# Nine small start-up loads of a four-layer cross-attention kernel issued from other engines' queues

## The reference, cut to what matters

```python
# layer 0: attention over the 256 features ("time"), 64 channels
Mn = Wn @ inorm(x) + bn;  Mm = Wm @ inorm(ctx) + bm;  Ml = Wl @ ctx + bl
A = softmax(einsum('bct,bcs->bts', Mn, Mm))
x = Wo @ einsum('bcs,bts->bct', Ml, A) + bo + x
# layers 1 and 2: 16 heads of 16 over the 64 rows, masked keys
a = layer_norm(ctx, ln_gamma, ln_beta)
Q, K, V = x @ Wq.T, a @ Wk.T, a @ Wv.T
x = x + tanh(gate) * (softmax(where(mask, Q K^T / 4, -inf)) V) @ Wo.T
# layer 3: one head of 256
x = x + alpha * (softmax((x w_q^T)(ctx w_k^T)^T / 16) (ctx w_v^T)) w_o^T
```

## Time and profile before

| | us |
|---|---|
| median of 3 runs | 601.56 |
| lowest, highest | 598.97, 601.84 |
| the profiled execution, device time | 601.84 |
| its span | 600.0 |
| PE busy in it | 564.3 (94%) |
| DVE, ACT, POOL busy | 473.7, 463.4, 120.5 |
| mean granted TensorE clock | 0.990 |
| start of PE's first matmul | 6.64 |
| start of `nT` on PE (L463), prologue | 21.65 |

### The profile page before, as it was taken

The page is one execution under the profiler, slowest core; times in us unless marked ns, Lnnn a source line. Parts: engine busy times, 40 slices in busy tenths (PEclk is TensorE's granted clock), DMA queues, the critical chain, the costliest instruction groups (busy, mean ns, idle before and its releaser), DMA issues.

```text
span 600.0 us, 26503 instructions
## 1 busy us (share of the span) xinstructions
PE 564.3 (94%) x11087; PEld 497.5 (83%) x11087; DVE 473.7 (79%) x1063; ACT 463.4 (77%) x961; POOL 120.5 (20%) x138
## 2 busy tenths in 40 slices
PE   3898999999999999999999999999999999999875
PEld 2687897988898897988889888988889888888864
DVE  4786969787897969878798869878797869877654
ACT  2675969878897869877797869878788778869661
POOL 8410070103410070102501060101601052000000
PEclk9989999999999999999999999999999999999979
DMA  9320000210021000210020100210020100010001
GB/s 218 107 77 2 2 3 14 68 38 2 2 78 34 7 2 3 78 37 2 2 78 3 37 2 2 78 38 2 2 78 2 38 1 3 3 38 1 2 3 36
DMA packets 18273, 18.36 MB, mean 31 GB/s; under 512 B 1552, under 2 KB 18064, under 8 KB 18176
## 3 DMA queue, kind: packets, MB, share of 16 engines
q1 hardware_dynamic: 17072, 16.19, 8.8%
q0 software_dynamic: 768, 0.45, 0.5%
q10 hardware_dynamic: 336, 0.20, 0.2%
HBM read 12.63 MB, written 4.19 MB: 28 GB/s over the span
## 4 chain that ended last, share of the span: by engine, by line
PE 76%; ACT 11%; DVE 6%; issue 4%; DVEq 0%; ACTq 0%
PE psum L383 13%; PE psum L673 11%; PE psum L727 10%; PE psum L385 10%; PE psum L384 10%; ACT work L854 5%; PE psum L720 5%; PE psum L640 4%; PE psum L653 3%; ACT v L803 3%; PE psum L520 2%; PE psum L463 2%; DVE shifted L1031 2%; PE psum L448 1%; DVE negmax L1027 1%
## 5 line engine op out<-in xcount | busy, mean ns | idle before, releaser
L1027 DVE TENSOR_REDUCE negmax<-psum 128x8 f32<-128x512 f32 x128 | 87.3, 682 | 11.2 <-PE psum L653 11.2
L1031 DVE TENSOR_TENSOR shifted<-psum,negmax 128x512 f32<-128x512 f32 x128 | 88.5, 692 | 5.3
L868 ACT ACTIVATE work<-psum,group_mask 128x512 f32<-128x512 f32 x128 | 80.4, 698 | 10.0 <-PE psum L673 9.6
L854 ACT ACTIVATE work<-shifted 128x512 f32<-128x512 f32 x128 | 75.5, 631 | 3.3 <-DVE shifted L1031 2.0
L673 PE MATMUL psum<-const,work 64*128 64x64 f32 x1536 | 64.9, 228 | 11.9 <-ACT work L854 9.2
L673 PEld LDWEIGHTS psum<-const,work 64*128 64x128 f32 x1536 | 56.2, 141 | 23.7 <-ACT work L854 14.9
L727 PEld LDWEIGHTS psum<-v,work 128*64 128x64 f32 x2048 | 63.0, 138 | 7.6 <-issue 3.0
L727 PE MATMUL psum<-v,work 128*64 128x34 f32 x2048 | 67.6, 225 | 0.8 <-ACT work L868 0.8
L803 ACT ACTIVATE v<-psum 64x256 f32<-64x256 f32 x128 | 49.6, 388 | 20.2 <-PE psum L385 19.1
L849 ACT ACTIVATE work<-psum,negmax 128x256 f32<-128x256 f32 x128 | 50.7, 483 | 3.8 <-DVE negmax L1023 3.7
L795 ACT ACTIVATE kbd<-psum,own_bias,const 128x512 f32<-128x512 f32 x64 | 46.6, 791 | 0.6 <-PE psum L385 0.6
(11 more groups left out here) (187 smaller groups left out, 1527.9 us busy)
## 6 DMA issues: line engine op xcount, KB each, us to landing
x_raw<-in_x_dram SPq DMA_DIRECT2D x8, 512.0 KB, 4.4
c_raw<-in_ctx_dram SPq DMA_DIRECT2D x8, 512.0 KB, 5.4
out_dram<-attn SPq DMA_DIRECT2D x16, 256.0 KB, 2.2
kbd<-in_L_xattn_Wq_dram SPq DMA_DIRECT2D x2, 256.0 KB, 9.0
kbd<-in_L_xattn_Wk_dram SPq DMA_DIRECT2D x2, 256.0 KB, 9.3
kbd<-in_L_xattn_Wv_dram SPq DMA_DIRECT2D x2, 256.0 KB, 10.2
kbd<-in_L_xattn_Wo_dram SPq DMA_DIRECT2D x2, 256.0 KB, 11.3
mrow_u<-in_mask_dram SPq DMA_DIRECT2D x7, 64.0 KB, 4.9
```

What stands on the lines that cost most here:

```text
L854: act.activation(probs[:, exp_row(g, l, i, last), :], shifted[:, i % 4, :], ACT.Exp).then_inc(exps, 1)
L868: act.activation(probsT[:, at, :], o[:], ACT.Copy, scale=group_mask[:, 2 * i + c:2 * i + c + 1]).then_inc(free, 1)
L1027: dve.tensor_reduce(negmax[:, i % 2, :], sv, AX_X, ALU.max, negate=True).then_inc(rowmax, 1)
L1031: dve.tensor_tensor(shifted[:, i % 4, :].rearrange("t (j k) -> t j k", k=C), sv, negmax[:, i % 2, :].unsqueeze(2).broadcast_to([P, NJ, C]) ...
```

## The change

Nine loads of the prologue are issued by another engine. The row mask `mrow_u8` goes from ACT to SP, ahead of the eight weights. The four layer-0 weights, the three layer-0 biases and `bo_row` go from POOL to ACT, behind `const`. What is loaded, from where and to where, and every wait on it are the same.

```diff
@@ sync
             sp.dma_start(x_raw[:], x_g[0]).then_inc(x_loaded, 16)
             sp.dma_start(c_raw[:], c_g[0]).then_inc(c_loaded, 16)
+            sp.dma_start(mrow_u8[:].rearrange("r p k -> r (p k)"),
+                         m_g[0].unsqueeze(0).broadcast_to([P, TOK])).then_inc(rows_loaded, 16)
             for l in (1, 2):
                 for n in "qkvo":
                     sp.dma_start(raw[f"{n}{l}"][:], w_in(w[f"L{l}_xattn_W{n}"])).then_inc(raw_loaded[f"{n}{l}"], 16)
@@ scalar
             act.dma_start(mask_u8[:], mask.rearrange("(p h) s -> p (h s)", h=2)).then_inc(mask_loaded, 16)
             act.dma_start(const[:], cst).then_inc(const_loaded, 16)
-            act.dma_start(mrow_u8[:].rearrange("r p k -> r (p k)"),
-                         m_g[0].unsqueeze(0).broadcast_to([P, TOK])).then_inc(rows_loaded, 16)
+            for i, n in enumerate(("Wn", "Wm", "Wo", "Wl")):
+                act.dma_start(w0_raw[:, i, :], w[f"L0_xattn_{n}"].unsqueeze(0).broadcast_to([2, C, C])).then_inc(w0_loaded, 16)
+            for i, n in enumerate(("bn", "bm", "bl")):
+                act.dma_start(scale_row[3 + 2 * NK + i:4 + 2 * NK + i, :].rearrange("r (h c) -> r h c", h=2),
+                              w[f"L0_xattn_{n}"].unsqueeze(0).unsqueeze(0).broadcast_to([1, 2, C])).then_inc(w0_bias_loaded, 16)
+            act.dma_start(bo_row, w["L0_xattn_bo"].unsqueeze(0).broadcast_to([P, C])).then_inc(bo_loaded, 16)
@@ gpsimd
             for n, name in enumerate(("L1_xattn_gate", "L2_xattn_gate", "L3_xattn_alpha")):
                 pool.dma_start(gate_in[n:n + 1, :], w[name].unsqueeze(0)).then_inc(gates_loaded, 16)
-            for i, n in enumerate(("Wn", "Wm", "Wo", "Wl")):
-                pool.dma_start(w0_raw[:, i, :], w[f"L0_xattn_{n}"].unsqueeze(0).broadcast_to([2, C, C])).then_inc(w0_loaded, 16)
-            for i, n in enumerate(("bn", "bm", "bl")):
-                pool.dma_start(scale_row[3 + 2 * NK + i:4 + 2 * NK + i, :].rearrange("r (h c) -> r h c", h=2),
-                              w[f"L0_xattn_{n}"].unsqueeze(0).unsqueeze(0).broadcast_to([1, 2, C])).then_inc(w0_bias_loaded, 16)
             for l in (1, 2):
                 for k in range(NK):
                     pool.dma_start(scale_row[3 + NK * (l - 1) + k:4 + NK * (l - 1) + k, :],
                                    w[f"L{l}_xattn_ln_gamma"][P * k:P * k + P].unsqueeze(0)).then_inc(gamma_loaded, 16)
-            pool.dma_start(bo_row, w["L0_xattn_bo"].unsqueeze(0).broadcast_to([P, C])).then_inc(bo_loaded, 16)
             for l in (1, 2):
                 pool.dma_start(beta_row[:, l - 1, :], w[f"L{l}_xattn_ln_beta"].unsqueeze(0).broadcast_to([P, D])).then_inc(beta_loaded, 16)
```

## The result

The changed kernel took 606.62 us in the median of four runs, against 600.82 for the kernel before, also of four: 5.8 us or 1.0% more. Over all 21 executions of the changed kernel on record (605.0 to 610.5, median 607.5) the ratio on record is 1.0118, 95% interval 1.0083 to 1.0154. The forecast was 601.4 with a range to 603.0, so it was wrong, and on the side that I had given 0.05. The profiled execution took 605.95 us with a span of 604.1.

What follows compares the result with a forecast made beforehand. PE's work in eight groups bounds the kernel, so only their start counts: profiled 601.84 - 0.15 us (norm_bias ending earlier) = 601.7, which lies 0.28 above the median, hence 601.4 us; eight in ten between 598.8 and 603.0.

Steps and rivals of the forecast that it cites:

- What bounds the kernel: Eight groups: bound by PE's own unchanged work, so the end moves by whatever their start at nT (21.65) moves.
- ACT's issues: Prologue, ACT: eight issues at 0.54 us each end at 6.1, upper bound 9.9; cost taken as 0.
- that cover: ACT in the prologue: xT.0's bank is next wanted by Wq2 at 15.41, 5 us after the 9.9 bound.
- The landing of what was moved: Layer-0 weights to DVE: no term in the sum; a DVE wait was only listed as a sign of being wrong.
- POOL's gain: Prologue, POOL: eight issues fewer save 5.3 us, 4.1 of them waiting for DVE; rstd 1.2 us earlier.
- `Wq2` and the third product: Prologue: Wq2 moves -2.2 to +1.9 us; rival: norm_bias waits for POOL's third product, +0.9 to +1.3 us, 602.5, chance 0.17.
- The lean of the sum: Wq2's load taken as +0.4 us, costing nothing up to +0.8; norm_bias shift -0.35 to +0.05, taken as -0.15.
- `norm_bias` held by the products: Prologue, DVE: norm_bias's 1.15 us was read as waiting for the end of a POOL product, 1.24 us each.
- `Wq2` early: Rival in the prologue: Wq2 lands by about 13.3, norm_bias saves 1.2 to 1.6 us; 600.0, chance 0.23.
- The slow stretch: DMA from 9 to 13 us at 175 against 383 GB/s; freeing it could give back up to 2.2 us.
- The page on issuing engines: Skill rule on DMA: the issuer saves only issuing time, so Wq2 stays at 15.41 and the sum is -0.15.
- The chances: Whole kernel, counted from 0.5%, 3.0 us: faster 0.08, slower 0.05, the same 0.87.

Runs made afterwards that it cites:

- e6: Changed kernel with each layer-0 weight loaded once, as 64 rows on ACT, both DVE spreading copies reading that half; median 602.88 us, ratio 1.0037.
- e3: Kernel before with only the four layer-0 weight loads moved to ACT, behind the row mask; median 606.32 us, ratio 1.0130.
- e1: Changed kernel with each layer-0 weight loaded by two 64-row transfers instead of one with a doubled source; median 605.09 us, ratio 1.0065.
- e7: Changed kernel with SP's weight loads held back until the layer-0 weights have landed; single run, 606.5 us.
- e2: Changed kernel with the four layer-0 weight loads put back on POOL behind the gates; median 604.81 us, ratio 1.0099.
- e5: Kernel before with each layer-0 weight loaded by two 64-row transfers on POOL; single run, 599.27 us.
- e10: e9 with POOL's four products also waiting for norm_bias; median 599.7 us, ratio 0.9965 against the kernel before.
- e8: Kernel before with each layer-0 weight loaded once, as 64 rows on POOL, both spreading copies reading that half; median 600.85 us, ratio 0.9996.
- e9: e8 with DVE's wait for the gates moved to just before its spreading copies; median 600.12 us, ratio 0.9960 against the kernel before.
- e4: Kernel before with only the row mask moved from ACT to SP; median 601.92 us, ratio 1.0015.

## Why the prediction was wrong, point by point

*What bounds the kernel.* Right: the groups ran as before, and the end moved with their start, 5.2 us at `nT` and, at the end, 4.1 in the profiled pair and 5.8 to 6.7 in the medians. It holds to about 2 us and no better: see e6.

*ACT's issues.* This step failed first. I took 0.54 us for each from one issue of one row, and as an upper bound one issue held as SP's was the earlier trace rows. They took 14.75 us together, and not even the bank stayed covered: `Wq2` waited for ACT until 18.50, as the prediction said it would if that cover went. The bound was of the wrong kind: three issues were held, one behind the other, and a bound on one is none on the sum. That a held issue waits for room in the ring of a busy engine is my reading of this; no run shows how much a ring takes, and the last three issues, behind the same weights, took 0.41 to 0.59 us. And the row that I took the price from moved a load whose pattern begins with 128 rows, whereas these begin with a repeated 2.

*The landing of what was moved.* This step was missing: the sum had no term for it, which put it at nothing. It is the one that cost the time, as e3 shows. The list of what would show the forecast wrong did name a wait of DVE for the layer-0 weights, but no rival had it and no time was given for it. I followed the loads that others wait for (`Wq2`, `ln_beta`) and the engines that issue, but not the moved loads themselves to their readers. The trace had the row. The last layer-0 weight of the kernel before:

```profile
5.48 0.83 POOL L1278 DMA_DIRECT2D scratch<-in_L_xattn_Wl_dram  x1
```

```profile
scratch<-in_L_xattn_Wl_dram POOLq DMA_DIRECT2D x1, 32.0 KB, 8.4
```

It landed at 13.9, and DVE's copies started at 14.20: 0.3 us of slack, and 1.1 more before `W0T` at 16.73, on loads which the change puts on another queue. It landed at 22.1 now, and that is +6.2 us on the start of `W0T` (16.73 to 22.94, with the biases). Two things made it late, and both were measured: the same bytes in 64-row loads landed at 16.5 behind the same loads of SP (e1), and the doubled loads without SP's weights at 11.9 (e7).

*POOL's gain.* Right in kind: of 5.3 us most went into waiting for DVE. Its first arithmetic waited for the mask columns until 10.73 (I had 9.7), `rstd` was done at 17.27 (I had 16.4), 0.3 us earlier than before and not 1.2. The gates landed 0.8 us later than before, more than the 0.5 that I had allowed. None of it mattered.

*`Wq2` and the third product.* In the changed kernel both were hidden: `Wq2`, issued at 4.88, landed 11.5 us later, at 16.4, while PE waited for ACT until 18.50. e2, the change without the layer-0 weights, shows them: `Wq2` 1.30 us later, within the -2.2 to +1.9, `norm_bias` held by the third product to 20.4, as that rival had it, and `nT` 1.1 us later. The lean of the sum, +0.4 for `Wq2`, was too small, and with it the forecast for this part had the wrong sign.

*`norm_bias` held by the products.* Right. It lasted 1.15, 0.77, 0.78, 1.23, 0.78 and 0.66 us where it came up during a product (before, e1, e2, e5, e6, e7) and 0.16 or 0.17 where none had begun yet or all were done, e10 by construction among them.

*`Wq2` early.* The slow stretch could indeed be freed, wholly by the form of the loads (341 GB/s in e8) and in part by who issues them (275 in the changed kernel, 287 in e3). In e3 `Wq2` came 1.05 us earlier. In the changed kernel it landed 1.0 us later all the same; that the loads issued earlier there (`ln_beta`, `bo_row`, the mask) were ahead of it is likely, and no run separates them.

*The page on issuing engines.* The Trainium skill (DMA: Bandwidth & Descriptors, "Issuing engines are not separate DMA queues") says that the same 16 engines do the work whoever issues, and e7 agrees: SP's weights on their own queue cost ACT's 10 us of landing. But I leaned on it for a landing that stays, and the change of the issuer moved that. The Trainium skill, in the same section, also calls the time to initiate a DMA usually small relative to the DMA itself. Here the eight issues took 14.75 us, of the 20.3 from the first issue (1.77) to the landing of the last weight.

*The chances.* With 0.05 for slower, the one rival on that side, the third product, reached 602.5 at most, and nothing on that side stood for the moved loads themselves. A move of eight loads to a queue that had none like them deserved a case of its own.

## What to carry to other kernels

Follow every moved load to its reader: when did it land before, how much later may it land, and what backlog is on the queue's engines now. Look at the dimension with which a small load begins, on both sides: with 64 rows or 128 it ran on 16 engines here, while a source repeated twice put four 32 KB loads on two engines and held the issuing engine for up to 4.5 us an issue, in front of its own arithmetic. Better still, don't load twice what an engine spreads afterwards anyway; by itself this gained nothing that ten runs can tell (e8), with the gates moved as well 0.4% (e9).

## What the runs showed that I had not expected

An issue of a DMA is not a fixed price: 0.41 to 4.46 us on ACT in one kernel. e1, with its weights on 16 engines, still took 0.62 to 2.08 us an issue from the fifth on; why it was held more than e6 (at most 1.15), with four loads and 320 packets more, is open.

The first load on ACT that begins with a 2, weight or bias, took 1.13 to 1.25 us to issue in all six kernels which have one (changed, e1, e2, e3, e6, e7), and the next one 0.52 to 0.84. In e2 it has two loads in front of it, so a full queue is hardly the reason; what it is, no run shows.

The time that a load takes depends on what else is queued: the doubled weights landed at 11.9 with SP's weights held back and at 22.1 with them.

Spreading copies of DVE took 0.29 us each with POOL idle (L1218, 0.59 for both in the changed kernel), 1.40 for both beside POOL's arithmetic before, and 2.69 beside its products in e1.

Executions of one kernel spread over up to 7 us (605.0 to 610.5 for the changed one, with a mean granted clock between 0.976 and 0.993; 598.0 to 605.1 for e4, with 0.969 to 0.992). In the profiles of before, changed, e1, e4 and e8 the clock falls below full at different places, all before 80 us and after 560. A difference of 1 or 2 us, as between `nT` in before, e4 and e8, doesn't come out of some ten runs, though the traces show it plainly.
